# An attention and feed-forward kernel whose attention stage stacks the two float16 halves on the partitions, with a new order of its step

## The chip, the cores and the metric

One core of a Trainium2 chip. The time is device time in microseconds (us) of one execution. Before the change it was 2286.6 us (median of 3 runs, 2283.81 to 2287.56). The profiled execution is a run of its own: 2283.59 us, of which 2281.9 are the span from its first to its last instruction. TensorE is PE in the rows (PEld its weight loads), VectorE is DVE, ScalarE ACT, GpSimd POOL, SyncE SP.

## What is computed

128 batches of 64 rows ("channels", S) by 1024 columns (T), float32; every batch has one of 16 conditions.

```
h    = einsum('bct,bcd->bdt', x, Wc[cond])       # 64 x 64 mix per batch
qkv  = h @ Wqkv + bqkv                           # 1024 -> 3 x 256
attn = softmax(q k' / 16)                        # 64 x 64 per batch
x    = x + (attn v) @ Wo + bo                    # 256 -> 1024
y    = x @ W2[cond]'                             # 1024 x 1024, one of 16
x    = x + y @ W' + b + lora(y)                  # lora: rank 8..64 by a gate's top 1
```

Every float32 operand is split in a float16 high half and a float16 low half (hi = f16(a), lo = f16(a - hi)); a product is hi*hi + hi*lo + lo*hi, three matmuls that add up in PSUM.

## The kernel before

**Two stages.** Stage A is everything up to `x1` (the attention), stage B the rest. Both take the batches in pairs: `NP` = 64 steps in each, four steps (q = 0 to 3) in one turn of a loop over i, 16 turns. `u = q // 2` is the group of four batches, `j = q % 2` the pair in it. In stage A the 64 channels of the two batches of a pair lie side by side on the 128 partitions or columns, and the mix and the attention are 128 x 128 products with zero blocks off the diagonal.

**One step of stage A.** `z_part` is x Wqkv of the *next* pair, 8 slices k of 6 matmuls with 384 columns. `z_hi` (ACT) and `z_lo` (DVE) split it. Then come for this pair, in this order: the mix to q and k (12 matmuls, `qkh`/`qkl` split it), the scores (6), mask, exponential and division (`sm`, `ex`, `pn`), the transposition, P' split in `pth` (ACT) and `ptl` (DVE), u = mix times P' (3), split in `uh` and `ul`, and o (6), split in `oh` and `ol`. TensorE fills the waits for these splits with slices of `z_part` (`zz(k)` in its program) and with the output products of the group before (`oo(n)`: 6 matmuls with 256 columns; on ACT `oo(n)` is the addition of the bias, L683, and on DVE the residual, L925). The first two steps have no group before them.

**Beside it.** ACT and DVE also split x of the pair after the next (`x_hi`, two operations, one for each batch, that signal once, after the second; `x_lo(.., 0)` and `x_lo(.., 1)`; the first slice of `z_part` waits for the second of these), the mix (`mix_hi`, `mix_lo`), and one unit of 1 MB of stage B's weights (`unit_hi`, `unit_lo`, L670 and L875), which SP loads to `stage` and stores again.

**What sets the order.** Each engine runs one program, written out by hand. It executes its instructions in this order, and a wait on a semaphore holds all that stand behind it on that engine. The orders on ACT and DVE in one step are

```
ACT  unit 0,1 | qkh x4 | mix_hi | unit 2 | oo(0) | ex | x_hi x2 | oo(1) | pth | oo(2) | uh | z_hi | oo(3) | oh
DVE  unit 0,1 | qkl x4 | mix_lo | oo(0) | sm | 1/sum, pn | unit 2 | x_lo 0 | oo(1) | ptl | x_lo 1 | oo(2) | ul | z_lo | oo(3) | ol
PE   zz(0,1) | mix | zz(2,3) oo(0) | scores | zz(4,5) oo(1) | transposition | zz(6) oo(2) | u | zz(7) oo(3) | o
```

**One step of stage B.** Four sets (`cond_set`) of 64 matmuls for y, split by `y_set`, the gate, and in every second step the FFN of the group before (`transposes`, `ffn`). The first products of the FFN need the last four weight units, which stay in SBUF (`unit_hi(IA, n, ..)`).

## Time and profile before

| what | value |
|---|---|
| median of 3 runs | 2286.6 us |
| profiled execution, its span | 2283.59 us, 2281.9 us |
| TensorE busy in the span, granted clock | 98%, 0.999 |
| DVE, ACT, POOL busy in the span | 54%, 42%, 3% |
| stage A, first z to the last output product | 10.56 to 798.0 us |
| stage B, first set to the end | 800.00 to 2281.9 us |
| TensorE in the chain that ended last | 96% |

Engines overlap: busy shares don't add up. The chain that ended last follows, from the last instruction back, what released each step.

### The profile page before, as it was taken

The numbers are of one execution on the slowest core, as the hardware profiler recorded it, in microseconds if no ns is written. First come the engines' busy times: TensorE is split into PE (matmuls) and PEld (weight loads), VectorE is DVE, ScalarE is ACT, GpSimd is POOL, SyncE is SP. The second block draws the span as 40 slices with busy tenths as digits, with TensorE's granted clock in tenths as the row PEclk, the third lists the DMA queues.
The fourth block names the chain that finished last, engine by engine and source line by source line (L and its number), as shares of the span: only waits on it lengthen the run. The fifth ranks groups of instructions, "written<-read, shape, count | busy, mean of one in ns | idle before, by whom it ended". The sixth has DMA issues, their size and how long they took to land.

```text
span 2281.9 us, 73807 instructions
## 1 busy us (share of the span) xinstructions
PE 2246.7 (98%) x28506; PEld 1748.9 (77%) x28506; DVE 1236.8 (54%) x3438; ACT 953.2 (42%) x2461; POOL 61.3 (3%) x128
## 2 busy tenths in 40 slices
PE   7999999999999889999999999999999999999998
PEld 4777777777777678887878787878787878787876
DVE  7777777777777754343434444444344444434443
ACT  5776767677767643232322222222222222222221
POOL 4000000000000000000000000000000000000000
PEclk9999999999999999999999999999999999999999
DMA  7668777777677743141214141214225132231303
GB/s 290 249 255 303 272 269 284 272 264 280 245 283 276 271 180 113 44 144 38 93 58 149 39 158 66 76 38 151 74 69 193 39 112 84 103 112 39 131 20 112
DMA packets 108960, 356.46 MB, mean 156 GB/s; under 512 B 27600, under 2 KB 28752, under 8 KB 79184
## 3 DMA queue, kind: packets, MB, share of 16 engines
q1 hardware_dynamic: 98640, 280.89, 34.1%
q0 software_dynamic: 10112, 72.36, 8.5%
q8 instruction: 184, 3.01, 0.5%
q14 instruction: 24, 0.20, 0.0%
HBM read 218.99 MB, written 134.22 MB: 155 GB/s over the span
## 4 chain that ended last, share of the span: by engine, by line
PE 96%; DVE 2%; DMA 1%; ACT 1%; issue 1%; POOL 0%; SPq 0%; DVEq 0%; ACTq 0%; POOLq 0%; PEldq 0%
PE bank L1179 21%; PE bank L1315 19%; PE bank L1284 19%; PE bank L1286 10%; PE bank L1317 10%; PE bank L1136 4%; PE bank L1138 4%; PE bank L1137 4%; PE bank L1297 1%; PE bank L1324 1%; PE bank L1325 1%; PE bank L1299 1%; DMA w<-ws 0%; DVE wf L875 0%; PE bank L1231 0%
## 5 line engine op out<-in xcount | busy, mean ns | idle before, releaser
L1284 PE MATMUL bank<-xs,w 128*128 128x128 f16 x8192 | 625.1, 219 | 3.9 <-DVE xs L882 2.0
L1179 PE MATMUL bank<-w,xs 128*128 128x384 f16 x3072 | 553.2, 327 | 4.4 <-DVE w L895 4.4
L1315 PE MATMUL bank<-y,wf 128*128 128x512 f16 x2048 | 483.8, 379 | 0.8 <-DVE xr L925 0.8
L1284 PEld LDWEIGHTS bank<-xs,w 128*128 128x128 f16 x8192 | 478.2, 98 | 5.8 <-issue 2.4
L763 ACT ACTIVATE zh<-bank 128x256 f32<-128x256 f32 x256 | 97.8, 382 | 777.1 <-PE bank L1286 774.1
L1179 PEld LDWEIGHTS bank<-w,xs 128*128 128x128 f16 x3072 | 290.6, 98 | 165.0 <-issue 2.8
L1286 PE MATMUL bank<-xs,w 128*128 128x64 f16 x8192 | 405.8, 193 | 0.0
L921 DVE SCALAR_TENSOR_TENSOR xr<-bank,xr 128x256 f32 (+1 forms) x256 | 108.6, 424 | 432.7 <-PE bank L1325 387.5
L1315 PEld LDWEIGHTS bank<-y,wf 128*128 128x128 f16 x2048 | 196.9, 98 | 186.6 <-DVE xr L925 1.1
L1286 PEld LDWEIGHTS bank<-xs,w 128*128 128x128 f16 x8192 | 335.9, 98 | 0.0
L1317 PE MATMUL bank<-y,wf 128*128 128x256 f16 x2048 | 265.4, 273 | 0.0
L1317 PEld LDWEIGHTS bank<-y,wf 128*128 128x128 f16 x2048 | 200.5, 98 | 77.7
L925 DVE SCALAR_TENSOR_TENSOR xr<-bank,xr 128x256 f32 (+1 forms) x512 | 216.0, 422 | 48.0 <-PE bank L1138 37.1
L1022 DVE SCALAR_TENSOR_TENSOR zl<-bank,zh 128x256 f32<-128x256 f32 x256 | 107.9, 422 | 244.8 <-ACT zh L763 244.8
L683 ACT ACTIVATE xr<-xr,bias (+1 forms) x512 | 237.7, 502 | 0.0
L765 ACT CAST y<-zl 128x256 f16<-128x256 f32 x256 | 103.7, 405 | 221.6 <-DVE zl L1022 221.6
L882 DVE SCALAR_TENSOR_TENSOR xs<-xr,xs 128x512 f16<-128x512 f16 (+1 forms) x256 | 170.3, 686 | 32.7 <-ACT xs L640 25.3
L1026 DVE TENSOR_TENSOR y<-zl,y 128x256 f16<-128x256 f32 x256 | 108.9, 425 | 120.5 <-ACT y L765 120.5
L875 DVE SCALAR_TENSOR_TENSOR wf<-stage,wf 128x512 f16<-128x512 f32 (+1 forms) x204 | 170.2, 864 | 1.3 <-ACT wf L670 1.3
L670 ACT ACTIVATE wf<-stage 128x512 f16<-128x512 f32 (+1 forms) x204 | 151.1, 784 | 0.0
L640 ACT ACTIVATE xs<-xr 128x512 f16 (+1 forms) x256 | 145.8, 616 | 4.5 <-DMA xr<-x_in 4.5
L1136 PE MATMUL bank<-oh,w 128*128 128x256 f16 x512 | 139.6, 273 | 2.6 <-DVE ol L995 1.4
(158 smaller groups left out, 2083.9 us busy)
## 6 DMA issues: line engine op xcount, KB each, us to landing
stage<-w_in SPq DMA_DIRECT2D x68, 1024.0 KB, 8.8
w<-ws POOLq DMA_DIRECT2D x68, 1024.0 KB, 6.1
ws<-wf SPq DMA_DIRECT2D x64, 1024.0 KB, 6.9
out<-xr SPq DMA_DIRECT2D x128, 256.0 KB, 2.3
xr<-x_in SPq DMA_DIRECT2D x31, 1024.0 KB, 8.0
x<-xr SPq DMA_DIRECT2D x31, 1024.0 KB, 4.4
xr<-x SPq DMA_DIRECT2D x124, 256.0 KB, 3.5
wcf<-wc_in SPq DMA_DIRECT2D x128, 32.0 KB, 4.5
```

The costliest lines, as they stand in the source:

```text
L640: last = nc.scalar.activation(split_view(q, b, 0), batch_view(i, q, b), Copy, scale=SX)
L670: nc.scalar.activation(unit_halves(q, final)[0][:, lo:hi], stage[:, q % 2, lo:hi], Copy, scale=SW).then_inc(s_wuh, 1)
L683: nc.scalar.activation(ring, ring, Iden, bias=bias[:, b0 + m:b0 + m + 1]).then_inc(s_ft, 1)
L875: v.scalar_tensor_tensor(out=low[:, lo:hi], in0=stage[:, q % 2, lo:hi], scalar=SW, in1=high[:, lo:hi], op0=ALU.mult, op1=ALU.subtract).the ...
L882: e = v.scalar_tensor_tensor(out=split_view(q, b, 1), in0=batch_view(i, q, b), scalar=SX, in1=split_view(q, b, 0), op0=ALU.mult, op1=ALU.s ...
L925: v.scalar_tensor_tensor(out=ring, in0=src[m % 2][:, 0:2 * P].rearrange("p (b s) -> p b s", b=4), scalar=scale, in1=ring, op0=ALU.mult, op ...
L1136: mm(dst, ah, bh, start=(k == 0), stop=False)
L1179: e = mm(zps[q % 2][h][:, 0:384], lhs, rhs[:, k, h * 384:(h + 1) * 384], start=(k == 0 and lhs is a and rhs is wq_h), stop=(k == K - 1 and ...
L1284: mm(both, hi[:, k, c], x_k, start=(k == 0), stop=False)
L1286: e = mm(y_m[:, at], lo[:, k, c], x_pair[:, k, at], start=False, stop=(k == K - 1))
L1315: mm(fps[m % 2][:, :], wf_h[:, k, c], yhl[:, u, k, :], start=(k == 0), stop=False)
L1317: mm(fps[m % 2][:, 0:2 * P], wf_l[:, k, c], yh[:, u, k, :], start=False, stop=False)
```

## The change

1. z is kept as `zs`: for each batch of the pair its high half lies on one half of the partitions and its low half on the other, with 64 of its channels in each. The mix `wch`/`wcl` is loaded twice, below itself, so that one matmul over 128 partitions gives hi*w + lo*w, and two of 64 columns (with `wch` and `wcl`) replace three of 128; P' is held in the same way (`pt`), and so is u, doubled. Mix 16 matmuls for 12, u 4 for 3, o 8 for 6, all with 64 columns; the scores stay. k goes to a part of z's own banks.
2. `z_hi` and `z_lo` go by batch: 64 partitions x 768 columns each, for 128 x 384. `pn` is made in two operations, `wch` and `wcl` are 384 columns wide for 256, and four DMAs bring the mix of a step for two.
3. A weight unit is split in four pieces of 512 columns, for 1024, 512, 512, and the order of the step is new on all three engines:

```
ACT  unit 0 | oo(0) | qkh x4 | mix_hi | unit 1,2 | ex | oo(1) | unit 3 | pt | oo(2) | x_hi x2 | uh | oo(3) | z_hi x2 | oh
DVE  unit 0 | qkl x4 | mix_lo | oo(0) | sm | unit 1 | 1/sum, pn x2 | unit 2 | oo(1) | pt | x_lo 0 | unit 3 | oo(2) | ul | x_lo 1 | z_lo x2 | oo(3) | ol
PE   zz(0,1,2) | mix | zz(3,4) oo(0) | scores | zz(5) oo(1) oo(2) | transposition | zz(6) oo(3) | u | zz(7) | o
```

4. Ends. At the start the second half of the first x is loaded after all eight slices of Wqkv, and its split and the first mix are made after them. TensorE's wait for the weights of the first output product and for the sort stands ahead of that product, no longer ahead of step 2. In stage B all four last weight units are split in step 0 (two after the first set, ahead of the other work; two at its end), no longer in steps 0 and 1. The last group is stored in three parts (`TAIL`: 4, 2 and 2 of 8 chunks), each when it is ready.

The core of the diff:

```diff
-PIECES = ((0, T), (T, T + T // 2), (T + T // 2, 2 * T))
+PIECES = tuple((n, n + T // 2) for n in range(0, PART * T, T // 2))
 NPC = len(PIECES)
+TAIL = ((0, 4), (4, 6), (6, 8))
...
-        zh_flat = sb("zh", [P, 2 * NQ], F16)
-        zl_flat = sb("zl", [P, 2 * NQ], F16)
-        zh = zh_flat[:, :].rearrange("p (r n) -> p r n", r=2)
-        zl = zl_flat[:, :].rearrange("p (r n) -> p r n", r=2)
+        zs_flat = sb("zs", [P, 2 * 2 * NQ], F16)
+        zs = zs_flat[:, :].rearrange("p (r b n) -> p r b n", r=2, b=2)
+        zs_two = zs_flat[:, :].rearrange("p (r b h n) -> p r b h n", r=2, b=2, h=2)
...
-        qkps, chps, wops = bank[4], bank[5], [bank[6], bank[7]]
+        zboth = [zbanks[:, 2 * n:2 * n + 2, 0:NQ // 2] for n in range(2)]
+        ZCOLS = ((0, NQ // 2), (NQ // 2, NQ))
+        qps, kps, chps, wops = bank[4], [bank[0], bank[2]], bank[5], [bank[6], bank[7]]
...
+        def qk_block(r, c):
+
+            return qps[:, c * P:(c + 1) * P] if c < 2 else kps[r][:, (c - 2) * P:(c - 1) * P]
...
-                    dst = wcf[b * S:(b + 1) * S, n, :].rearrange("p (t d) -> p t d", t=2)[:, :, b * S:(b + 1) * S]
-                    src = wc_in[bass.ds(e, 1), :, :, :].rearrange("a c t d -> (a c) t d")
-                    sp.dma_start(dst, src).then_inc(s_wc[n], 16)
+                    for half in range(2):
+                        sp.dma_start(wcf[half * S:(half + 1) * S, n, 3 * b * S:3 * (b + 1) * S],
+                                     wc_in[bass.ds(e, 1), :, :].rearrange("a c n -> (a c) n")).then_inc(s_wc[n], 16)
...
             def z_hi(i, q):
 
                 wait(act, s_z, i, 4, q + 1)
-                for h in range(2):
-                    e = nc.scalar.activation(zh[:, q % 2, h * 384:(h + 1) * 384], zps[q % 2][h][:, 0:384], Copy,
-                                             scale=SZ / (SX * SW))
-                e.then_inc(s_zh, 1)
+                for b in range(2):
+                    at = slice(b * S, (b + 1) * S)
+                    nc.scalar.activation(zs_two[at, q % 2, b, :, :], zboth[q % 2][at, :, :], Copy,
+                                         scale=SZ / (SX * SW)).then_inc(s_zh, 1)
...
-                    unit_hi(i, q, (0, 1))
+                    unit_hi(i, q, (0,))
+                    oo(0)
...
-                unit_hi(i, q, (0,) if end else (2,))
-                oo(1 if end else 0)
+                unit_hi(i, q, (0,) if end else (1, 2))
+                if end:
+                    oo(1)
                 wait(act, s_sm, i, 4, q + 1)
                 nc.scalar.activation(ex[:, :], sm[:, :], ACT.Exp, bias=soft[:, 0:1], scale=-1.0,
                                      accum_out=soft[:, 1:2]).then_inc(s_e, 1)
+                if end:
+                    oo(2)
+                else:
+                    oo(1)
+                    unit_hi(i, q, (3,))
+                wait(act, s_t, i, 4, q + 1)
+                nc.scalar.copy(pt[0:S, :], chps[0:S, 0:P]).then_inc(s_pth, 1)
+                if end:
+                    unit_hi(i, q, (1, 2))
+                if end:
+                    oo(3)
+                else:
+                    oo(2)
                 if not (last and q >= 2):
                     x_hi(i, q + 2)
-                oo(2 if end else 1)
-                wait(act, s_t, i, 4, q + 1)
-                nc.scalar.copy(pth[:, :], chps[:, 0:P]).then_inc(s_pth, 1)
-                if end:
-                    unit_hi(i, q, (1,))
-                oo(3 if end else 2)
                 wait(act, s_u, i, 4, q + 1)
                 nc.scalar.activation(uh[:, :], chps[:, 0:P], Copy, scale=SU / (SC * SP)).then_inc(s_uh, 1)
                 if end:
-                    unit_hi(i, q, (2,))
+                    unit_hi(i, q, (3,))
                 else:
+                    oo(3)
                     z_hi(i, q + 1)
-                    oo(3)
...
+                if first and q == 0:
+                    for n in range(2):
+                        unit_hi(IA, n, range(NPC), n)
                 y_set(i, q, 1)
-                if not (last and q == 3):
-                    x_hi(i, q + 1, phase_b=True)
                 if first and q == 0:
                     chunk_hi(K + 4)
                     chunk_hi(K + 5)
+                if not (last and q == 3):
+                    x_hi(i, q + 1, phase_b=True)
                 y_set(i, q, 2)
                 y_set(i, q, 3)
-                if first and q < 2:
-                    for n in range(2 * q, 2 * q + 2):
+                if first and q == 0:
+                    for n in range(2, 4):
                         unit_hi(IA, n, range(NPC), n)
...
             def z_lo(i, q):
-                wait(dve, s_zh, i, 4, q + 1)
-                for h in range(2):
-                    c = slice(h * 384, (h + 1) * 384)
-                    e = v.scalar_tensor_tensor(out=zl[:, q % 2, c], in0=zps[q % 2][h][:, 0:384],
-                                               scalar=SZ / (SX * SW), in1=zh[:, q % 2, c], op0=ALU.mult,
-                                               op1=ALU.subtract)
-                e.then_inc(s_zl, 1)
+                for b in range(2):
+                    wait(dve, s_zh, i, 8, 2 * q + b + 1)
+                    at, other = slice(b * S, (b + 1) * S), slice((1 - b) * S, (2 - b) * S)
+                    v.scalar_tensor_tensor(out=zs_two[other, q % 2, b, :, :], in0=zboth[q % 2][at, :, :],
+                                           scalar=SZ / (SX * SW), in1=zs_two[at, q % 2, b, :, :], op0=ALU.mult,
+                                           op1=ALU.subtract).then_inc(s_zl, 1)
...
+                if not end:
+                    unit_lo(i, q, (1,))
                 wait(dve, s_e, i, 4, q + 1)
                 v.reciprocal(soft[:, 2:3], soft[:, 1:2]).then_inc(s_r, 1)
                 wait(dve, s_r, i, 4, q + 1)
-                v.tensor_scalar(pn[:, :], ex[:, :], soft[:, 2:3], SP, ALU.mult, ALU.mult).then_inc(s_p, 1)
-                if not end:
+                for b in range(2):
+                    at = slice(b * S, (b + 1) * S)
+                    block = ex[at, at].rearrange("p (a n) -> p a n", a=1).to_broadcast([S, 2, S])
+                    e = v.tensor_scalar(pn[at, :, :], block, soft[at, 2:3], SP, ALU.mult, ALU.mult)
+                e.then_inc(s_p, 1)
+                if end:
+                    oo(2)
+                else:
                     unit_lo(i, q, (2,))
+                    oo(1)
+                wait(dve, s_pth, i, 4, q + 1)
+                v.tensor_tensor(pt[S:P, :], chps[0:S, 0:P], pt[0:S, :], ALU.subtract).then_inc(s_ptl, 1)
                 if not (last and q >= 2):
                     x_lo(i, q + 2, 0)
-                oo(2 if end else 1)
-                wait(dve, s_pth, i, 4, q + 1)
-                v.tensor_tensor(ptl[:, :], chps[:, 0:P], pth[:, :], ALU.subtract).then_inc(s_ptl, 1)
+                if end:
+                    unit_lo(i, q, (1, 2))
+                    oo(3)
+                else:
+                    unit_lo(i, q, (3,))
+                    oo(2)
+                wait(dve, s_uh, i, 4, q + 1)
+                v.scalar_tensor_tensor(out=ul[:, :], in0=chps[:, 0:P], scalar=SU / (SC * SP), in1=uh[:, :],
+                                       op0=ALU.mult, op1=ALU.subtract).then_inc(s_ul, 1)
                 if not (last and q >= 2):
                     x_lo(i, q + 2, 1)
                 if end:
-                    unit_lo(i, q, (1,))
-                oo(3 if end else 2)
-                wait(dve, s_uh, i, 4, q + 1)
-                v.scalar_tensor_tensor(out=ul[:, :], in0=chps[:, 0:P], scalar=SU / (SC * SP), in1=uh[:, :],
-                                       op0=ALU.mult, op1=ALU.subtract).then_inc(s_ul, 1)
-                if end:
-                    unit_lo(i, q, (2,))
+                    unit_lo(i, q, (3,))
                 else:
                     z_lo(i, q + 1)
                     oo(3)
...
-                zz(0, 1)
+                zz(0, 1, 2)
                 if not more:
                     oo(0)
 
-                wait(pe, s_zl, i, 4, q + 1)
                 wait(pe, s_wcl, i, 4, q + 1)
-                for c in range(4):
-                    d = slice(c * P, (c + 1) * P)
-                    e = three(qkps[:, d], [(zh[:, r, d], zl[:, r, d], wch[:, r, 0:P], wcl[:, r, 0:P])])
+                wait(pe, s_zl, i, 8, 2 * q + 2)
+                for b in range(2):
+                    at = slice(b * S, (b + 1) * S)
+                    mix = slice((3 * b + 2) * S, (3 * b + 3) * S)
+                    for c in range(4):
+                        dst, z_c = qk_block(r, c)[:, at], zs[:, r, b, c * P:(c + 1) * P]
+                        mm(dst, z_c, wch[:, r, mix], start=True, stop=False)
+                        e = mm(dst, z_c, wcl[:, r, mix], start=False, stop=True)
                 e.then_inc(s_qk, 1)
                 if not more:
                     pe.wait_ge(s_z, NP)
                     pe.sem_inc(s_c2, TS - 1)
-                zz(2, 3)
+                zz(3, 4)
                 oo(0 if more else 1)
 
                 wait(pe, s_qkl, i, 4, q + 1)
                 wait(pe, s_ol, i, 4, q)
                 three(chps[:, 0:P], [(qkh[:, c, :], qkl[:, c, :], qkh[:, 2 + c, :], qkl[:, 2 + c, :])
                                      for c in range(2)]).then_inc(s_s, 1)
-                zz(4, 5)
-                oo(1 if more else 2)
+                zz(5)
+                if more:
+                    oo(1)
+                oo(2)
                 wait(pe, s_p, i, 4, q + 1)
-                nc.tensor.transpose(chps[:, 0:P], pn[:, :], ident[:, :]).then_inc(s_t, 1)
+                nc.tensor.transpose(chps[:, 0:P], pn[:, :, :].rearrange("p a n -> p (a n)"), ident[:, :]).then_inc(s_t, 1)
                 zz(6)
-                oo(2 if more else 3)
+                oo(3)
 
                 wait(pe, s_ptl, i, 4, q + 1)
-                three(chps[:, 0:P], [(wch[:, r, P:2 * P], wcl[:, r, P:2 * P], pth[:, :], ptl[:, :])]).then_inc(s_u, 1)
+                for b in range(2):
+                    at = slice(b * S, (b + 1) * S)
+                    for half, w in enumerate((wch, wcl)):
+                        twice = w[:, r, 3 * b * S:(3 * b + 2) * S]
+                        e = mm(chps[:, at], twice, pt[:, at], start=(half == 0), stop=(half == 1))
+                e.then_inc(s_u, 1)
                 zz(7)
-                if more:
-                    oo(3)
 
                 wait(pe, s_ul, i, 4, q + 1)
-                for c in range(2):
-                    d = slice(2 * DH + c * P, 2 * DH + (c + 1) * P)
-                    e = three(chps[:, c * P:(c + 1) * P], [(zh[:, r, d], zl[:, r, d], uh[:, :], ul[:, :])])
+                for b in range(2):
+                    at = slice(b * S, (b + 1) * S)
+                    for c in range(2):
+                        dst = chps[:, c * P + b * S:c * P + (b + 1) * S]
+                        z_c = zs[:, r, b, 2 * DH + c * P:2 * DH + (c + 1) * P]
+                        mm(dst, z_c, uh[:, at], start=True, stop=False)
+                        e = mm(dst, z_c, ul[:, at], start=False, stop=True)
                 e.then_inc(s_o, 1)
```

## Rows read from the trace of the kernel before

**Rows 1.** Busy time of the engines in the even part of stage A (start:end, length).
```profile
120.00:768.00 648.00, 648.00 (x5384) 463.79 (x5383) 500.76 (x1295) 456.67 (x1184) 1.59 (x3) 1.00 0.74 271
```

**Rows 2.** Timeline of TensorE, one step: start, length, line, out<-in, count.
```profile
408.14 2.11 PE L1179 MATMUL bank<-w,xs 128*128 128x384 f16 x12
...
410.09 0.22 PE L1136 MATMUL bank<-wch,zh 128*128 128x128 f16 x1
...
416.30 0.27 PE L1231 MATMUL bank<-ident,pn 128*128 128x128 f32 x1
...
418.04 0.22 PE L1136 MATMUL bank<-pth,wch 128*128 128x128 f16 x1
...
419.84 0.22 PE L1136 MATMUL bank<-uh,zh 128*128 128x128 f16 x1
...
420.17 2.11 PE L1179 MATMUL bank<-w,xs 128*128 128x384 f16 x12
```

**Rows 3.** Timeline of ACT in the same step, from the exponential's end.
```profile
414.89 1.13 ACT L640 ACTIVATE xs<-xr 128x512 f16 x2
415.93 0.49 ACT L683 ACTIVATE xr<-xr,bias  x1
416.61 0.27 ACT L723 CAST pth<-bank 128x128 f16<-128x128 f32 x1 [0.19 <-PE bank L1231]
416.77 0.51 ACT L683 ACTIVATE xr<-xr,bias  x1
418.41 0.28 ACT L728 ACTIVATE uh<-bank 128x128 f16<-128x128 f32 x1 [1.12 <-PE bank L1138]
419.38 0.87 ACT L689 ACTIVATE zh<-bank 128x384 f16<-128x384 f32 x2 [0.70 <-PE bank L1179]
```

**Rows 4.** Timeline of DVE in the same step.
```profile
416.24 0.69 DVE L882 SCALAR_TENSOR_TENSOR xs<-xr,xs 128x512 f16<-128x512 f16 x1
416.85 0.42 DVE L925 SCALAR_TENSOR_TENSOR xr<-bank,xr 128x256 f32 x1
417.19 0.28 DVE L979 TENSOR_TENSOR ptl<-bank,pth 128x128 f16<-128x128 f32 x1
417.38 0.68 DVE L882 SCALAR_TENSOR_TENSOR xs<-xr,xs 128x512 f16<-128x512 f16 x1
...
418.76 0.28 DVE L986 SCALAR_TENSOR_TENSOR ul<-bank,uh 128x128 f16<-128x128 f32 x1
420.29 1.02 DVE L932 SCALAR_TENSOR_TENSOR zl<-bank,zh 128x384 f16<-128x384 f32 x2 [1.25 <-ACT zh L689]
```

**Rows 5.** Timeline of TensorE in stage B: matmuls with 128 and 64 columns.
```profile
1203.15 0.61 PE L1284 MATMUL bank<-xs,w 128*128 128x128 f16 x8
1203.60 0.40 PE L1286 MATMUL bank<-xs,w 128*128 128x64 f16 x8
1203.83 0.61 PE L1284 MATMUL bank<-xs,w 128*128 128x128 f16 x8
```

**Rows 6.** Timeline of ACT and DVE in stage B: six unit pieces (two with 1024 columns).
```profile
814.32 4.08 ACT L670 ACTIVATE wf<-stage 128x1024 f16<-128x1024 f32 x6
...
815.41 4.76 DVE L875 SCALAR_TENSOR_TENSOR wf<-stage,wf 128x1024 f16<-128x1024 f32 x6 [0.53 <-ACT wf L670]
```

**Rows 7.** Timeline of SP's queue: the loads of two steps' mixes, and a unit's load.
```profile
417.34 4.85 SPq L332 DMA_DIRECT2D wcf<-wc_in  x4
...
423.11 0.35 SPq L352 DMA_DIRECT2D stage<-w_in  x1
```

**Rows 8.** The page's DMA issues: unit loads (count, size, median us to landing).
```profile
stage<-w_in SPq DMA_DIRECT2D x68, 1024.0 KB, 8.8
```

**Rows 9.** Timeline: TensorE at step 2 and at the first FFN, and SP's last stores.
```profile
47.02 2.12 PE L1179 MATMUL bank<-w,xs 128*128 128x384 f16 x12 [2.28 <-DVE w L895]
...
839.51 0.28 PE L1305 MATMUL bank<-ident,mhl 128*128 128x128 f16 x2 [2.75 <-DVE mhl L1082]
...
2277.35 1.93 SPq L453 DMA_DIRECT2D out<-xr  x4
```

More of the change, by code:

```diff
@@ L484, in _ @@
             body_b(IB - 1, last=True)
-            store_out(IB - 1, 1)
-            for u in range(2):
-                sp.wait_ge(s_out[u], 64 * IB)
+            rs = batches(IB - 1, 1)
+            for lo, hi in TAIL:
+                sp.wait_ge(s_res, FA + 16 * IB - K + hi)
+                for b, r in enumerate(rs):
+                    sp.dma_start(out[bass.ds(r, 1), :, lo * S:hi * S].rearrange("a p n -> (a p) n"),
+                                 group_cols(GB - 1, b * BT + lo * S, (hi - lo) * S)).then_inc(s_out[1], 16)
+            sp.wait_ge(s_out[0], 64 * IB)
+            sp.wait_ge(s_out[1], 64 * (IB - 1 + len(TAIL)))
         @block.gpsimd
@@ L904, in _ @@
                     link(dve_copy(2, UPTO, trps[0:NC, 0:1]))
-                if n == 5:
-                    mix_lo(0, 0)
-                if n == 6:
-                    for b in range(2):
-                        x_lo(0, 1, b)
+            mix_lo(0, 0)
+            for b in range(2):
+                x_lo(0, 1, b)
             def residual(i, u, ms, phase_b=False):
@@ L1094, in b_step @@
                     gating(pi, pu, 1)
+                if first and q == 0:
+                    for n in range(2):
+                        unit_lo(IA, n, range(NPC), n)
                 y_set(i, q, 1)
+                if first and q == 0:
+                    chunk_lo(K + 4)
+                    chunk_lo(K + 5)
                 if j == 0 and before:
@@ L1100, in b_step @@
                         x_lo(i, q + 1, b, phase_b=True)
-                if first and q == 0:
-                    chunk_lo(K + 4)
-                    chunk_lo(K + 5)
                 y_set(i, q, 2)
                 y_set(i, q, 3)
-                if first and q < 2:
-                    for n in range(2 * q, 2 * q + 2):
+                if first and q == 0:
+                    for n in range(2, 4):
                         unit_lo(IA, n, range(NPC), n)
@@ L1258, in _ @@
             a_step(0, 1)
-            pe.wait_ge(s_wl, K + 4)
-            pe.wait_ge(s_sort, S_SEGMENTS + 1)
             a_step(0, 2)
```

52 lines of the change are left out of this document (28 added, 24 removed).

## Prediction

> **What bounds the kernel now.** I read the windows by stage first: in the even part of stage A TensorE is busy for the whole 648 us while DVE works 501 and ACT 457 [rows 1]. So the stage goes at TensorE's pace, and the question is what a step costs it. The timeline of TensorE gives that: a step runs from one `zz(0,..)` to the next, 408.14 to 420.17, 12.03 us [rows 2]. Twelve z matmuls take 410.09 - 408.14 = 1.95 us, 0.1625 each, so the 48 of a step take 7.80. From u to o (418.04 to 419.84) lie 3 small matmuls, a z slice (0.98) and an output product; a small one takes 0.056 (eight in 1203.60 - 1203.15 = 0.45 [rows 5]), which leaves 0.66 for the product, 2.6 for four. The 27 small ones take 1.5 and the transposition 0.11 (418.04 - 416.30 less 0.98 and 0.65). Sum 12.0: the step has no hole. I then read the timelines of ACT and DVE for how far the splits are from holding TensorE: `ptl` ends at 417.47 for a u at 418.04, `ul` at 419.04 for an o at 419.84, `z_lo` at 421.31 for a mix after 422.1 [rows 2, 4]. The slack is 0.6 to 0.8 us each time. Stage B is bound by TensorE too, and the change touches only its first step and its end.
>
> **Part 1, the stacked halves.** Out go 12 + 3 + 6 = 21 matmuls of 128 columns, 21 x 0.056 = 1.17 us. In come 16 + 4 + 8 = 28 of 64. Stage B has this form: eight take 1203.83 - 1203.60 = 0.23 us, each with a weight load of its own, 0.029 each [rows 5]; 28 x 0.029 = 0.81. TensorE's work falls by 0.36 us a step, to 11.67. The bounds of a 64-column matmul are 0.029 and the 0.056 of the 128-column one (if small ones in long rows don't stay as fast as between wide ones); I take 0.029, the row of the same shape.
>
> The Trainium skill (TensorE: Matmul & The Clock Gate, Back-to-back issue gap) speaks against this part: it gives a sustained 81 ns for matmuls of 128 columns, and about 62 ns for each of up to 64 where the sequencer decodes them. By that 28 would cost 1.74 us and the change would add 0.57 a step instead of saving 0.36. The trace disagrees at 128 columns (56 ns) and has 29 ns at 64 [rows 5].
>
> **Part 2, wider splits.** `z_lo` takes 1.02 us for two operations of 384 columns, one 0.55, and `z_hi` 0.87 [rows 3, 4]. With 768 columns I scale by columns, less the fixed part that two operations of different width show: about 0.95 and 0.82 each, so DVE gets 0.8 us more and ACT 0.7; `pn`, `wch`/`wcl` and the fourth piece add some 0.4 on DVE. DVE had 147 us idle in 648, 2.7 a step [rows 1], so it would still fit in 11.67, with 1.2 to spare. Nothing here is on TensorE's path by itself: z ends with `zz(7)`, the last `z_lo` some 2.8 us later, and o plus three slices cover 3.2. The cover is thin (0.4), and if it is gone each 0.1 costs 6 us.
>
> **Part 3, the order.** This decides. A wait holds all that stands behind it on its engine, so I follow the chain from the transposition's issue (time 0) to o. TensorE: 0.11, z slice to 1.09, product to 1.74, u (4 x 0.029) to 1.86, `zz(7)` to 2.84. It could issue o at 2.84; before, one more product (0.66) stood there.
> - ACT: `pt` starts 0.31 after the transposition (416.61 - 416.30), and the next operation 0.16 later [rows 2, 3]. The bias of `oo(2)` holds it 0.4 (0.51, of which 0.1 overlaps with the next, as in the two of 0.61 that take 1.13). *Then* come the two `x_hi`, formerly right behind the exponential. They start at 0.87 and end 1.13 later [rows 3], at 2.00.
> - DVE: `pt`'s low half is done by 0.8, and then `x_lo(.., 0)` waits for `x_hi`, which signals only at 2.00. Before, at 416.24, it had been ready. Behind it on DVE stand unit piece 3, the residual of `oo(2)`, and `ul`. They start at 2.04, 2.65 (416.85 - 416.24 = 0.61), 3.25 (0.60: four such and two of double width take 4.76 [rows 6]) and 3.59 (0.34 = 417.19 - 416.85) [rows 4]. `ul` takes 0.28, with a handoff of 0.04 o can go at 3.91.
>
> TensorE waits 3.91 - 2.84 = 1.07 us for `ul`. o takes 0.23, until 4.14. The next step's `zz(0)` needs `x_lo(.., 1)`, which now stands behind `ul`: start 3.83, end 4.51 (0.68), TensorE at 4.55, a second wait of 0.41. The z chain is then covered: the second `z_lo` ends near 6.3, the mix is due at 4.55 + 2.93 = 7.48. The softmax has 0.98 + 1.31 = 2.3 us of cover for 2.6 before; `unit 1` between the mask and 1/sum uses up 0.1 there, and it ends some 0.3 before it is due.
>
> Per step: -0.36 + 1.07 + 0.41 = +1.12 us. It holds in steps 2 to 61 (before them there is no group before, and the last two don't split x): 60 x 1.12 = **+67 us**. By 0.056 for a 64-column matmul only the mix (16) and u or o outside the waits count, +0.4 a step, +24 us.
>
> **DMAs.** Two steps' mixes take SP 4.85 us for four issues [rows 7]; eight issues take at least four more times some 0.5, about 2.2 us. The unit load behind them (423.11, 8.8 us to landing [rows 7, 8]) landed near 432 for a use just after 433. It comes 2.2 later against a deadline that moves by 2.2 to 2.4 with the longer steps, and ACT's first piece has 2 us of room: nothing, at most 0.5 a pair of steps, 15 us.
>
> **Part 4, the ends.** Start: steps 0 and 1 have no output products to hide the shorter covers, their waits (softmax, `ul`) grow by about 0.6 each, less 0.36; the wait of 2.28 at step 2 [rows 9] goes, and 0.4 for `x_lo` comes in its place: about -1.4. Wqkv's slices already arrive as TensorE needs them: 0. Stage B, step 0: eight unit pieces (8 x 0.53 on ACT, 8 x 0.6 = 4.8 on DVE [rows 6]) now stand ahead of the split of the next x, and `y_set(1, 0)` waits behind two more units whose load depends on SP. That costs step 1 and 2 some 1.5 to 5 us; in return the hole of 2.75 before the first FFN [rows 9] closes. Bounds -2.75 and +6; I take +2. End: four issues of 1.93 stay behind the last chunk [rows 9], but move a quarter of the bytes: -0.5, between 0 and -1.5.
>
> **Sum.** 67 - 1.4 + 2 - 0.5 = +67 us on the profiled execution's 2283.6, 2351; the median of the runs is 3.0 above it, so **2354 us**, 2.9% slower. No change means within 0.2%, 4.6 us, of 2286.6.
>
> **The rivals.**
> - *No wait: the savings stay* (faster). If `x_hi` and what follows were quick enough, stage A would give 61 x 0.36 = 22 us, and the sum is about 2265. The point that decides is the time from transposition to o: at 2.84 it is hidden, and the step gets no slower until 3.2 (the 0.36 saved, with the second wait then gone). The chain gives 3.91 from eight durations of the same operations, so it would have to be 18% wrong; the unseen ones (64 partitions instead of 128) aren't long in it. Chance 0.13. In between, same time: 0.03.
> - *64-column matmuls don't go at 0.029* and the waits come on top: 2354 + 24 = 2378. Only the row of stage B speaks, where eight wide ones stand between eight narrow ones. Chance 0.13.
> - *The unit's load or DVE becomes the bound*: DVE has 10.5 us of work in 13.1, the load is near its deadline; up to +15, 2365 to 2370. Chance 0.06.
> - The forecast, 2354: chance 0.65, own range 2338 to 2368 (an error of 0.2 us in the waits is 12 us).
>
> Slower 0.65 + 0.13 + 0.06 = 0.84, same 0.03, faster 0.13. The range leaves out the faster side and what is beyond the second rival: 2335 to 2386.
>
> **What the profile after would show.** A step of 13.1 us in stage A; TensorE idle about 1.1 us before o, released by DVE `ul`, and 0.4 before `zz(0)`, released by DVE `xs`; DVE idle 1.2 us before the first `x_lo`, released by ACT `xs`; no wait before the mix; TensorE's share in stage A near 89%. Starts 0.029 apart in the mix show part 1 right. A step of 11.7 with no hole would make the prediction wrong, a wait before the mix would show part 2 wrong.

## The result and the profile after

The changed kernel takes 2366.73 us (median of 4 runs, 2366.17 to 2368.0) against 2286.69 for the kernel before on the same chip: a ratio of 1.0354, 95% interval 1.0343 to 1.0366. It is slower, as forecast, and 12.7 us slower than the 2354 that were forecast. The profiled execution took 2366.17, its span is 2364.5.

The page after, its first part, and the windows of the even part of stage A (start:end, length, then busy us and count on PE, PEld, DVE, ACT and POOL, granted clock, DMA share, GB/s):

```profile
span 2364.5 us, 75251 instructions
...
PE 2249.7 (95%) x28954; PEld 1730.1 (73%) x28954; DVE 1329.6 (56%) x3570; ACT 1021.8 (43%) x2529; POOL 60.1 (3%) x128
```
```profile
120.00:840.00 720.00, 648.75 (x5765) 445.38 (x5763) 577.88 (x1405) 515.28 (x1244) 1.59 (x3) 1.00 0.70 253
```

TensorE was busy all the time in stage A [rows 1]; now it is for 90% of it, at full granted clock, and no other engine is near its bound. So there are waits. To see where, I took the issue of the transposition as the mark of each step. Its first and last issue in the part that should be even, steps 2 and 61, after the change:

```profile
54.66 0.27 PE L1274 MATMUL bank<-ident,pn 128*128 128x128 f32 x1
...
842.87 0.27 PE L1274 MATMUL bank<-ident,pn 128*128 128x128 f32 x1
```

That is 788.21 us for 59 steps, 13.359 each. Before, the same marks stood at 55.20 and 765.36: 12.037 each. The whole difference of the spans, 82.6 us:

| part | before | after | difference |
|---|---|---|---|
| start to the transposition of step 2 | 55.20 | 54.66 | -0.5 |
| 59 steps to that of step 61 | 710.16 | 788.21 | +78.0 |
| two more steps | 22.08 | 23.23 | +1.15 |
| last transposition to the first set of stage B | 12.56 | 14.16 | +1.6 |
| first set to the first FFN | 39.51 | 44.06 | +4.55 |
| first FFN to the last residual's end | 1437.2 | 1436.4 | -0.8 |
| last residual's end to the span's end | 5.17 | 3.75 | -1.4 |

Most steps take 13.27 or 13.35. Four take 14.32, 13.61, 13.48 and 13.93; there ACT waits up to 1.8 us for the DMA of the mix. One step, timelines of TensorE, ACT and DVE after the change; "[1.05 <-DVE ul L1015]" is the idle time before an instruction and what ended it:

```profile
415.94 0.27 PE L1274 MATMUL bank<-ident,pn 128*128 128x128 f32 x1
...
417.80 1.14 PE L1213 MATMUL zbanks<-w,xs 128*128 128x384 f16 x6
419.99 0.20 PE L1293 MATMUL bank<-uh,zs 128*128 128x64 f16 x1 [1.05 <-DVE ul L1015]
...
420.58 3.10 PE L1213 MATMUL zbanks<-w,xs 128*128 128x384 f16 x18 [0.19 <-DVE xs L905]
423.52 0.19 PE L1256 MATMUL bank<-wch,zs 128*128 128x64 f16 x1
423.55 0.19 PE L1257 MATMUL bank<-wcl,zs 128*128 128x64 f16 x1
```
```profile
416.25 0.26 ACT L738 CAST pt<-bank 64x128 f16<-64x128 f32 x1 [0.47 <-PE bank L1274]
416.42 0.51 ACT L693 ACTIVATE xr<-xr,bias  x1
416.83 1.14 ACT L652 ACTIVATE xs<-xr 128x512 f16 x2
```
```profile
416.77 0.28 DVE L1005 TENSOR_TENSOR pt<-bank,pt 64x128 f16<-64x128 f32 x1
418.10 0.69 DVE L905 SCALAR_TENSOR_TENSOR xs<-xr,xs 128x512 f16<-128x512 f16 x1 [1.05 <-ACT xs L652]
418.71 0.68 DVE L898 SCALAR_TENSOR_TENSOR wf<-stage,wf 128x512 f16<-128x512 f32 x1
419.31 0.42 DVE L946 SCALAR_TENSOR_TENSOR xr<-bank,xr 128x256 f32 x1
419.65 0.28 DVE L1015 SCALAR_TENSOR_TENSOR ul<-bank,uh 128x128 f16<-128x128 f32 x1
419.85 0.68 DVE L905 SCALAR_TENSOR_TENSOR xs<-xr,xs 128x512 f16<-128x512 f16 x1
```

Read from the top: `pt` 0.31 after the transposition, the bias of `oo(2)` behind it, then `x_hi` until 417.97. DVE idles 1.05 us for that, and only then come `x_lo(.., 0)`, unit piece 3, the residual and `ul`. The last slice of z takes 0.98, so TensorE could issue o at 418.78; it does at 419.99, 1.21 us late (in every second step 1.30), and the next `zz(0)` waits another 0.35 for `x_lo(.., 1)` (eight o matmuls from 419.99 take 0.23, the slice comes at 420.58). The idle time in the brackets counts from the modelled end of the matmul before and is smaller than such a gap between issues; the gaps are used here. The first mix matmul comes without a wait, 2.94 after `zz(0)`, and the matmuls of 64 columns are 0.03 apart.

### The profile page after: what moved, and what is told of

The parts are those of the page before. It is cut to its first block, busy times and chain, and to the rows that moved or that the text cites. A ratio compares the mean times of both kernels' runs of the same rounds, so it can differ in the third digit from the quotient of the medians.

```text
span 2364.5 us, 75251 instructions
## 1 busy us (share of the span) xinstructions
PE 2249.7 (95%) x28954; PEld 1730.1 (73%) x28954; DVE 1329.6 (56%) x3570; ACT 1021.8 (43%) x2529; POOL 60.1 (3%) x128
## 4 chain that ended last, share of the span: by engine, by line
PE 84%; DVE 5%; issue 3%; ACT 3%; DMA 3%; SPq 2%; DVEq 1%; ACTq 0%
PE zbanks L1332 19%; PE bank L1363 19%; PE zbanks L1213 15%; PE zbanks L1334 10%; PE bank L1365 9%; ACT xs L652 2%; PE bank L1170 2%; PE bank L1171 2%; PE bank L1172 2%; DVE xs L905 2%; PE bank L1345 1%; PE bank L1372 1%; PE bank L1373 1%; DVE xr L946 1%; DVE wf L898 1%
## 5 line engine op out<-in xcount | busy, mean ns | idle before, releaser
L1332 PE MATMUL zbanks<-xs,w 128*128 128x128 f16 x8192 | 627.6, 220 | 8.3 <-DVE xs L905 8.3
L1213 PE MATMUL zbanks<-w,xs 128*128 128x384 f16 x3072 | 553.4, 327 | 14.8 <-DVE xs L905 12.8
L1332 PEld LDWEIGHTS zbanks<-xs,w 128*128 128x128 f16 x8192 | 480.4, 98 | 10.2 <-issue 8.8
L1213 PEld LDWEIGHTS zbanks<-w,xs 128*128 128x128 f16 x3072 | 285.0, 98 | 182.1 <-DVE xs L905 16.7
L1334 PE MATMUL zbanks<-xs,w 128*128 128x64 f16 x8192 | 406.9, 193 | 0.0
L1334 PEld LDWEIGHTS zbanks<-xs,w 128*128 128x128 f16 x8192 | 337.0, 98 | 0.0
L1053 DVE SCALAR_TENSOR_TENSOR zs<-zbanks,zs 128x256 f32<-128x256 f32 x256 | 108.1, 422 | 246.6 <-ACT zs L783 246.6
L785 ACT CAST y<-zs 128x256 f16<-128x256 f32 x256 | 103.6, 405 | 219.7 <-DVE zs L1053 219.7
L898 DVE SCALAR_TENSOR_TENSOR wf<-stage,wf 128x512 f16<-128x512 f32 x272 | 185.6, 686 | 6.3 <-ACT wf L680 4.0
L1057 DVE TENSOR_TENSOR y<-zs,y 128x256 f16<-128x256 f32 x256 | 108.9, 425 | 120.5 <-ACT y L785 120.5
L680 ACT ACTIVATE wf<-stage 128x512 f16<-128x512 f32 x272 | 162.5, 630 | 5.5 <-DMA stage<-w_in 5.5
```

The costliest lines, as they stand in the source:

```text
L680: nc.scalar.activation(unit_halves(q, final)[0][:, lo:hi], stage[:, q % 2, lo:hi], Copy, scale=SW).then_inc(s_wuh, 1)
L898: v.scalar_tensor_tensor(out=low[:, lo:hi], in0=stage[:, q % 2, lo:hi], scalar=SW, in1=high[:, lo:hi], op0=ALU.mult, op1=ALU.subtract).the ...
L1213: e = mm(zps[q % 2][h][:, 0:hi - lo], lhs, rhs[:, k, lo:hi], start=(k == 0 and lhs is a and rhs is wq_h), stop=(k == K - 1 and lhs is b))
L1332: mm(both, hi[:, k, c], x_k, start=(k == 0), stop=False)
L1334: e = mm(y_m[:, at], lo[:, k, c], x_pair[:, k, at], start=False, stop=(k == K - 1))
```

## The experiments

Ratios are to the kernel before on the same chip, with 95% intervals. "Step" is the mean from the transposition of step 2 to that of step 61: 12.037 before, 13.359 in the change. The theory under test: both waits come from places in the queues of ACT and DVE. The rivals: TensorE waits because DVE has too much work, or because of the stacked halves themselves, or for a DMA.

**1. `x_hi` early again.** One group of lines moved on ACT, for the first wait.

```diff
                 nc.scalar.activation(ex[:, :], ...)
+                if not (last and q >= 2):
+                    x_hi(i, q + 2)
...
                     oo(2)
-                if not (last and q >= 2):
-                    x_hi(i, q + 2)
                 wait(act, s_u, i, 4, q + 1)
```

> The changed kernel with one edit: on ACT the two x_hi stand right behind the exponential again, all else as changed. Theory (the late x_hi holds DVE's queue, and with it ul): the wait before o falls from 1.29 us to some 0.25 (unit piece 3, still between exponential and P' on DVE's way), the one before the first z slice stays near 0.4; a step of about 12.4 us for 13.34, so 2311 us. Rival 1 (the wider splits overload ACT and DVE): moving work of the same length changes little, step above 13, 2350 or more. Rival 2 (SP's loads are late): no change.

Measured: 2325.8 us, 1.0172 (1.0155 to 1.0189), step 12.68: a clear gain, but 15 us less than the 2311 expected. TensorE and DVE in one of its steps:

```profile
440.22 1.14 PE L1213 MATMUL zbanks<-w,xs 128*128 128x384 f16 x6
441.79 0.20 PE L1293 MATMUL bank<-uh,zs 128*128 128x64 f16 x1 [0.42 <-DVE ul L1015]
...
442.38 0.82 PE L1213 MATMUL zbanks<-w,xs 128*128 128x384 f16 x4 [0.19 <-DVE xs L905]
```
```profile
439.52 0.28 DVE L1005 TENSOR_TENSOR pt<-bank,pt 64x128 f16<-64x128 f32 x1
439.90 0.69 DVE L905 SCALAR_TENSOR_TENSOR xs<-xr,xs 128x512 f16<-128x512 f16 x1
440.51 0.69 DVE L898 SCALAR_TENSOR_TENSOR wf<-stage,wf 128x512 f16<-128x512 f32 x1
441.11 0.42 DVE L946 SCALAR_TENSOR_TENSOR xr<-bank,xr 128x256 f32 x1
441.45 0.28 DVE L1015 SCALAR_TENSOR_TENSOR ul<-bank,uh 128x128 f16<-128x128 f32 x1
```

DVE's idle time before `x_lo(.., 0)` is gone, and the gap before o falls from 1.21 to 441.79 - 440.22 - 0.98 = 0.59, where 0.25 was expected. The move of two instructions is worth half of the loss. The other half of the first wait is three operations that stand between `pt` and `ul` on DVE, and 0.38 from `pt` to the next start where before it was 0.19 from `ptl` [rows 4].

**2. `x_lo(.., 0)` behind `ul`.** The same wait, from the other side: DVE's queue changes, `x_hi` stays late.

```diff
                 v.tensor_tensor(pt[S:P, :], ...).then_inc(s_ptl, 1)
-                if not (last and q >= 2):
-                    x_lo(i, q + 2, 0)
...
                 if not (last and q >= 2):
+                    x_lo(i, q + 2, 0)
                     x_lo(i, q + 2, 1)
```

> The changed kernel with one edit: on DVE x_lo(.., 0) moves from behind P' to behind ul, next to x_lo(.., 1); ACT as changed. Theory: ul no longer stands behind the wait for x_hi, so the wait before o goes; both x_lo now stand between ul and the next step's first z slice, and the wait there grows from 0.36 to about 0.9 us. Step about 12.65 us, 2326 us. Rival 1 (DVE has too much work): the same work in the same step, no gain, above 2350. Rival 3 (the lateness of x_hi as such, not what is queued behind it): no gain either.

Measured: 2328.57 us, 1.0188 (1.0171 to 1.0205), step 12.72, within 3 us of what was expected. Timeline of TensorE:

```profile
439.46 1.14 PE L1212 MATMUL zbanks<-w,xs 128*128 128x384 f16 x6
440.43 0.19 PE L1292 MATMUL bank<-uh,zs 128*128 128x64 f16 x1
...
441.70 1.47 PE L1212 MATMUL zbanks<-w,xs 128*128 128x384 f16 x8 [0.87 <-DVE xs L905]
```

o follows its slice with no gap, and the wait now stands before z, for the second `x_lo`: 441.70 - 440.43 - 0.23 = 1.04. DVE's amount of work is that of the change in both runs, and each saves some 0.65 us a step. DVE's load is not the cause of the first wait; the queue is.

**3 and 4. One half of the change each.** Experiment 3 has the stacked halves with the old order on all three engines and the old pieces of the unit (1024, 512, 512). Experiment 4 is the kernel before with the new order and four pieces:

```diff
-PIECES = ((0, T), (T, T + T // 2), (T + T // 2, 2 * T))
+PIECES = tuple((n, n + T // 2) for n in range(0, PART * T, T // 2))
...
-                if not (last and q >= 2):
-                    x_hi(i, q + 2)
-                oo(2 if end else 1)
...
+                    oo(2)
+                if not (last and q >= 2):
+                    x_hi(i, q + 2)
```

> Parts 1 and 2 alone: stacked halves, wider splits, four mix loads, with the order of the step and the three unit pieces of the kernel before (the ends as changed). If the stacking is a gain that the new order throws away, a step takes 11.67 us, 2286.7 - 60 x 0.36 + 4 = 2269 us. My walk through the queues says otherwise: with two z slices of cover the second z_lo ends when the mix is due or just after, everything behind it on DVE is later by 0.8 us, and ql is late for the scores by 0.6: step about 12.35, 2286.7 + 60 x 0.32 + 4 = 2310 us. Rival 1 (wider splits are the whole cause) says near 13.3, 2366.

> Part 3 alone: the kernel before with the new order of the step on ACT, DVE and TensorE and four unit pieces; products, narrow splits, two mix loads and the ends as before. Theory (the order is the cause): both waits are there, 1.0 to 1.3 before o and 0.35 before the first z slice, on top of the larger work of 12.01; step 13.4 us, 2286.7 + 60 x 1.4 = 2371 us. Rival 1 (wider splits): step at 12.0 to 12.1, about 2287 to 2292.

(The diff is of 4; 3 keeps its lines as they were before, and takes `zs`, `wch`/`wcl`, `pt` and the doubled u from the change. It also keeps the ends of the change, its new start of stage B among them, and one edit that the list of the change leaves out: `qkh` signals after two of its four operations, so that DVE starts on `qkl` earlier. Experiment 4 has the ends of the kernel before.) Measured: 3 takes 2333.61 us, 1.0208 (1.0191 to 1.0225), step 12.80; 4 takes 2375.66, 1.0393 (1.0376 to 1.041), step 13.54. Timelines of DVE and TensorE in experiment 4:

```profile
451.47 0.69 DVE L891 SCALAR_TENSOR_TENSOR xs<-xr,xs 128x512 f16<-128x512 f16 x1 [1.26 <-ACT xs L640]
```
```profile
453.35 0.23 PE L1152 MATMUL bank<-uh,zh 128*128 128x128 f16 x1 [1.00 <-DVE ul L1000]
```

The order alone has the same two waits, and costs 1.5 us a step, a little more than expected. The stacking takes 0.18 of that away again. Alone, in the old order, it is no saving either. A cost of 0.3 was expected (a step of 12.35, 2310 us); it is 0.76, 0.66 in most steps (12.70) and the rest in a few long ones. DVE and TensorE in experiment 3:

```profile
444.12 0.28 DVE L994 TENSOR_TENSOR pt<-bank,pt 64x128 f16<-64x128 f32 x1
444.43 0.69 DVE L896 SCALAR_TENSOR_TENSOR xs<-xr,xs 128x512 f16<-128x512 f16 x1
...
446.90 1.94 DVE L944 SCALAR_TENSOR_TENSOR zs<-zbanks,zs 64x768 f16<-64x768 f32 x2 [1.13 <-ACT zs L700]
448.88 0.42 DVE L937 SCALAR_TENSOR_TENSOR xr<-bank,xr 128x256 f32 x1
...
449.86 1.83 DVE L889 SCALAR_TENSOR_TENSOR wf<-stage,wf 128x1024 f16<-128x1024 f32 x2
451.61 0.60 DVE L965 SCALAR_TENSOR_TENSOR qkl<-bank,biasq,qkh 128x128 f16<-128x128 f32 x2
```
```profile
451.87 0.27 PE L1156 MATMUL bank<-oh,w 128*128 128x256 f16 x1
452.78 0.23 PE L1154 MATMUL bank<-qkh 128*128 128x128 f16 x1 [0.64 <-DVE qkl L965]
```

`z_lo` takes 1.94 us instead of 1.02 [rows 4], and in the old order two unit pieces, a residual and `ol` stand between it and `qkl`. So `qkl` is late, and the first score waits 452.78 - 451.87 - 0.11 = 0.80 us. The mix waits too, 0.20 us, until `z_lo` ends: the 12 matmuls of its two slices start at 446.75 and take 1.95, it comes at 448.90. The two waits less the 0.36 saved are the 0.64 of most steps. This is read from the trace; no run takes these operations away in the old order, and none has the stacking without the wider splits. The old order has no room for the wider splits here, the new one has (no wait before mix or scores), but it opens the two waits at `ul` and `x_lo`.

**5. Both orders mended.** The stacked halves, with this order behind the exponential: ACT `x_hi` x2, `oo(1)`, `pt`, `oo(2)`, unit 3, `uh`; DVE `pt`, `x_lo` 0, `x_lo` 1, `ul`, `oo(2)`, unit 3, `z_lo`. DVE's part of the diff:

```diff
                     x_lo(i, q + 2, 0)
+                    x_lo(i, q + 2, 1)
...
-                else:
-                    unit_lo(i, q, (3,))
-                    oo(2)
...
                 v.scalar_tensor_tensor(out=ul[:, :], ...).then_inc(s_ul, 1)
-                if not (last and q >= 2):
-                    x_lo(i, q + 2, 1)
...
+                if not end:
+                    oo(2)
+                unit_lo(i, q, (3,))
```

> The changed kernel, same work and same order on TensorE, with the orders of ACT and DVE mended: x_hi right behind the exponential, unit piece 3 behind the bias of oo(2) on ACT; on DVE both x_lo right behind P', then ul, then the residual of oo(2) and unit piece 3 ahead of z_lo. By the walk through the queues with the measured durations no wait of TensorE is left, the smallest slack being 0.1 us (ul for o, z_lo for the mix). Theory: step at TensorE's work, 11.67 to 11.75, 2366.7 - 60 x 1.63 = 2269 us, faster than both kernels. Rival 1 (the wider splits are too much for ACT and DVE): a step above 12.0, 2288 or more, with DVE busy without a hole.

Measured: 2295.73 us, 1.0042 (1.0027 to 1.0058), where 2269 was expected. Most steps take 11.68 to 11.78, as expected, which is TensorE's own work (11.67). But the mean is 12.165: every fourth takes 12.2, and of the early ones every eighth 14.5 to 16.4. Timelines of ACT and of SP's queue just ahead of a step of 12.24:

```profile
460.29 0.52 ACT L658 ACTIVATE wch<-wcf 128x384 f16<-128x384 f32 x1 [0.87 <-DMA wcf<-wc_in]
```
```profile
453.64 7.21 SPq L338 DMA_DIRECT2D wcf<-wc_in  x8
```

With the queues of ACT and DVE in order, ACT waits for the mix 28 times, up to 4.38 us. Not all of the 12.24 is that: 0.34 of it stands before the first z slice of the next turn of the loop, which experiment 11 has too. The waits suggest SP as the next bound: two steps' mixes are eight issues of 7.2 us where four took 4.85 [rows 7]. Experiments 7 to 11 try that.

**6. Old start of stage B.** The change, but with the last weight units split where they were before.

```diff
-                if first and q == 0:
-                    for n in range(2):
-                        unit_hi(IA, n, range(NPC), n)
                 y_set(i, q, 1)
...
+                if first and q < 2:
+                    for n in range(2 * q, 2 * q + 2):
```

> The changed kernel with one edit: in the first steps of stage B the last four weight units are split where the kernel before did it. In the change, first set to first FFN takes 44.1 us for 39.5, with two holes of TensorE of 3.66 and 2.79 us, after each of which matmuls go at half speed for some 3 us. Theory: with the old placing the first hole shrinks to about 1.8 and the second goes, a hole of 2.75 before the FFN comes back, matmuls stay at full speed, and the stretch takes 39.5: 2362 us. If the holes come from the loads of the slots instead, nothing changes: 2367.

Measured: 2361.73 us, 1.0335 (1.0321 to 1.0349); stage A as in the change (13.359). Windows from the first set to the first FFN, 44.06 us in the change and 37.79 here (879.17 to 916.96; the window is a little wider):

```profile
880.26:924.32 44.06, 37.61 (x801) 37.36 (x802) 26.76 (x66) 21.25 (x48) 0.01 (x1) 0.92 0.53 203
```
```profile
879.00:917.00 38.00, 34.94 (x801) 34.42 (x802) 25.63 (x66) 20.72 (x48) 0.18 (x1) 1.00 0.66 235
```

The new placing costs 6.3 us there, more than the 4.55 that the table shows against the kernel before. In that kernel TensorE waited 1.80 us for a DMA of weights at 810.14, a wait that neither the change nor experiment 6 has. The same 801 matmuls are busy for 37.61 us instead of 34.94, which is the granted clock (0.92), 2.7 us; the rest, 44.06 - 37.61 against 38.00 - 34.94, are 3.4 us more of holes. They stand before sets that wait for the split of the next x, which the units in step 0 hold up.

**7 to 11. The DMAs.** Two edits, each tried on the change and on the mended order (that of 5, with the old start of stage B). The first, "ahead": SP issues the mixes ahead of the load of x; the load of the next unit stays behind both. The second, "two loads": the mix lies twice below itself in HBM, so that one DMA to 128 partitions does for two, four issues for two steps as before.

```diff
                 for u in range(2):
+                    for j in range(2):
+                        q = 2 * u + j
+                        if not (last and q >= 2):
+                            load_mix(i, q + 2)
...
-                    for half in range(2):
-                        sp.dma_start(wcf[half * S:(half + 1) * S, n, 3 * b * S:3 * (b + 1) * S],
+                    sp.dma_start(wcf[:, n, 3 * b * S:3 * (b + 1) * S],
```

> e5_both_orders_mended, with the old placing of the units in stage B, and SP issuing the mix loads ahead of the load of x. Theory: effects add: 2269 - 4.5 - 2 to 3 = 2262 us, 1.1% faster than the kernel before. If the loads of units are late with the shorter step (SP's eight mix loads take 7.1 us for 4.85), ACT's first unit piece waits for its DMA and a step stays at 12 or above: 2280 or more.

> The changed kernel with one edit: SP issues a group's mix loads ahead of its load of x. In the change four of the first 32 steps take 0.1 to 1.0 us longer (14.32 for 13.35 the longest), where ACT waits up to 1.8 us for the mix. Theory (the eight issues of 7.1 us come too late behind the x load): these peaks go, 2 us in all, 2364.5 us. Rival: the peaks come from the traffic of the first condition's weights and stay: 2367.

> e5_both_orders_mended with the old placing of the units in stage B, SP's order as in the change, and the mix of a step brought by two DMAs of 128 partitions for four of 64 (the mix lies twice in HBM). In e5_both_orders_mended most steps take 11.7 us, but their mean is 12.17: every eighth some takes 14.5, every fourth 12.2, where ACT waits up to 3.6 us for the mix, and SP's eight issues take 7.1 us. Theory (SP's queue is the new bound): with four issues of 4.9 us the waits for the mix go but for the smallest, mean step 11.75, 2295.7 - 59 x 0.42 - 4.5 = 2267 us, below both kernels. If it is the DMA traffic and not SP's queue, little changes: 2290.

> The changed kernel with that edit alone: two mix loads of 128 partitions for four of 64. The peaks of some steps (14.32, 13.61, 13.48, 13.93 for 13.35) go, about 2 us: 2364.5. It prices the four loads in the changed kernel, where the long step hides them.

> e9_two_mix_loads with one edit: SP issues the four mix loads ahead of its load of x, right behind the odd step's unit load. In e9_two_mix_loads a step's mean is still 12.08: every eighth step up to half way takes 14.2 to 15.6 and every fourth 12.05, and ACT waits 0.3 to 3.5 us for the mix there. Theory: the mixes are then landed a step earlier and all their peaks go, as they went with this edit alone in the changed kernel; the unit load comes 5 us earlier than in e7_all_mended, 53 us instead of 57 on its clock, lands in 10 us and is in time. Mean step 11.72, 2284.9 - 59 x 0.36 = 2264 us. If the unit loads are late again (as in e7_all_mended, each fourth step at 13.4), 2280 or more.

| kernel | edits | median us | ratio (95%) | step |
|---|---|---|---|---|
| 8 | change, ahead | 2363.32 | 1.0341 (1.0326, 1.0355) | 13.323 |
| 10 | change, two loads | 2363.86 | 1.0342 (1.0328, 1.0356) | 13.323 |
| 7 | mended, ahead | 2290.92 | 1.0022 (1.0012, 1.0031) | 12.232 |
| 9 | mended, two loads | 2284.92 | 0.9998 (0.9989, 1.0007) | 12.08 |
| 11 | mended, both | 2271.64 | 0.994 (0.9926, 0.9954) | 11.831 |

On the change the DMAs are worth 3 us of 80: in 8 and in 10 the four long steps vanish, (13.359 - 13.323) x 59 = 2 us. On the mended order each edit alone comes out 18 to 29 us above the lower number of its expectation. Of what 7 and 9 have below experiment 5, 8 and 5 us come from the old start of stage B (first set to first FFN 37.79 and 40.78 us for 45.93). In the steps the edit of 7 by itself costs (12.232 - 12.165) x 59 = 4 us, and that of 9 saves 5: half the issues alone don't cure the waits. ACT still waits 16 times for the mix in 9, up to 4.25 us, and its 2285 is nearer to the expectation's second case (2290) than to its first. In 7 the step is as the expectation's second case has it, and the wait moves to ACT's unit piece. The unit's load now stands right behind that of x and takes 10.3 us to land (from 456.92) where it took 6.7 in experiment 5. ACT and SP's queue in 7:

```profile
467.22 0.63 ACT L680 ACTIVATE wf<-stage 128x512 f16<-128x512 f32 x1 [2.43 <-DMA stage<-w_in]
```
```profile
467.33 1.00 SPq L359 DMA_DIRECT2D stage<-w_in  x1
470.37 8.37 SPq L338 DMA_DIRECT2D wcf<-wc_in  x8
```

With both, the unit's load is issued some 3 us earlier in its step than in 7, takes as long to land, and is in time but for six waits of ACT (5.25 us in all, the longest 2.64 at 120.48, in a step of 13.34); no wait for the mix is left. Experiment 11, windows of four steps, and its o and next z:

```profile
430.00:477.22 47.22, 47.05 (x430) 32.75 (x429) 43.06 (x105) 37.87 (x94) 0.00 (x0) 1.00 0.81 283
```
```profile
434.85 1.14 PE L1200 MATMUL zbanks<-w,xs 128*128 128x384 f16 x6
435.90 0.20 PE L1280 MATMUL bank<-uh,zs 128*128 128x64 f16 x1
...
436.14 3.09 PE L1200 MATMUL zbanks<-w,xs 128*128 128x384 f16 x18
```

TensorE is busy all the time again, with 435.90 - 434.85 - 0.98 = 0.07 before o; DVE is at 91%, so little more would fit. 11 is faster than both kernels, 14.3 us below the one before beside it (2285.93), and 7.6 above what was expected. Its every fourth step still takes 12.05. These steps are the last of each turn of the loop: there the first z slice of the next turn comes 0.34 to 0.39 us late (at 400.91 for one), and the profile names no releaser for it, only "issue". The same 0.34 stands at the end of most turns in experiments 5, 7 and 9, and at no other step. So it is no wait for a split or a DMA that the profile shows. The kernel before has its turns without it; why is open.

## Why the prediction was right, and where it was off

- **TensorE's work, -0.36 a step: right.** 16 mix matmuls take 0.47, 0.029 each, and steps with no wait take 11.68 (experiments 5 and 11) for a forecast of 11.67. The rival with the slower matmuls of 64 columns was priced at 56 ns each; the runs show 29. The Trainium skill (TensorE: Matmul & The Clock Gate, Back-to-back issue gap) has about 62 ns for them where the sequencer decodes them; this trace does not show such a limit.
- **The first wait, the decisive step: right, 0.14 to 0.23 short.** 1.07 forecast, 1.21 and 1.30 measured in turn. Experiments 1 and 2 take away what makes it, from either side, and it falls by half or goes. Of the chain, in the step shown, `x_hi` ended at 2.03 for 2.00; but `x_lo` started 0.13 behind it, not 0.04, and the unit, the residual and `ul` at 2.77, 3.37 and 3.71 for 2.65, 3.25 and 3.59. The handoff to o was 0.34 from `ul`'s start, against 0.32. The term that was too small is the handoff from ACT to DVE, 0.09 of the 0.14: it was taken as 0.04, and over the 59 steps it is 0.14 in the median (0.10 to 0.23). Why every second step has 0.09 more is open.
- **The second wait: right.** 0.41 forecast, 0.35 measured. Its sum with the first, 1.25 in the mean, less 0.36, gives 1.24 and a step of 13.28; most take 13.27 or 13.35.
- **60 steps: 67 forecast, 78.0 measured over 59 intervals.** (13.323 - 12.037) x 59 = 76 come from the even steps, by the step of experiments 8 and 10, which have no long ones; that is 0.17 a step more than forecast. The other 2 come from the four long ones.
- **Part 2: sizes and cover right in the new order.** The two `z_lo` take 1.94 (0.95 each forecast), and `z_hi` 1.63 (0.82 each). No wait stands before the mix. In the old order it does not hold: 0.20 stand before the mix and 0.80 before the scores (experiment 3), a case that the prediction had no reason to look at.
- **DMAs: right in size, not in place.** Forecast were 0 to 15 us and a late load of the unit; measured are 2 us by the long steps, 3 by experiments 8 and 10, and ACT waits there for the mix. The eight issues took 7.2 us for a forecast of 7.1. The longer steps hid the rest; in the mended order it came to 20 us, (12.165 - 11.831) x 59 between experiments 5 and 11, with fewer issues and their new place together.
- **The turn to stage B: mis-sized.** +2 forecast for the start of stage B, +4.55 measured, inside the bounds. The places are those named: the hole of 2.75 before the FFN went, and steps 1 and 2 got holes of 3.66 and 2.79, 6.45 together for the 1.5 to 5 forecast. The clock's fall, some 2.8 us more, was not in the sum; nor was the wait of 1.80 that went. The end of stage A had no term and gave +1.6. TensorE waits there for `ul` (1.27, for 1.02 before) and `ol` (1.36, as before), and its clock falls: output matmuls stand 0.21 apart for some 3 us instead of 0.11. Most of the 1.6 is that fall: experiment 8 has the same two waits, its clock stays at 1.00, and the stretch takes 12.79 for 14.16.
- **The ends.** Start -0.5 for -1.4, end -1.4 for -0.5; they cancel.
- **The other rivals.** "No wait" needed o within 3.2 us of the transposition; it came at 4.05 to 4.13. That DVE becomes the bound fell with experiment 2, in which the same work goes faster; it is busy for 80% of stage A. For the unit's load ACT waited once, 0.56 us.
- **The sum.** In the profiled execution it was 15.5 us short (2366.2 for 2350.7): 9 in the even steps, 2 in the long ones, 5.3 at the turn to stage B, 0.9 at the start, less 0.8 in the rest of stage B and 0.9 at the end. The median lay 0.6 above this execution instead of 3.0, which leaves 13.0 (12.7 against the rounded 2354). That the two ends cancel is luck.

## What to carry to other kernels

Before an operation is moved in an in-order queue, walk the chain of every value whose producer now stands behind it, on both engines: two `x_hi` moved from ahead of the transposition's split to behind it held up four DVE operations, and the waits cost four times what the shorter products saved (1.6 against 0.36 us a step). Moving the two back gave half of it; the other half was in DVE's own order. A shorter form of the products and the order around it must be judged together: here the stacking in the old order cost 2.1% (with the new ends), the order alone 3.9%, both 3.5%, and the same stacking with its producers ahead of what waits, its loads in fewer issues and ahead of x, and the old start of stage B gained 0.6%. A cost that is hidden (here of the loads) comes back when the waits that hid it are mended, so try an edit on the kernel in which its cover is gone, and together with its partner: of the two edits to the loads one alone cost 4 us and the other saved 5, both saved 20.
